# Graph stage: rows of f2 scores by transposing one more column of h1 and h2, in place of 512-column products

## The reference, cut to what matters

```
h = inp @ W
f1 = h @ a[:F, 0]
f2 = h @ a[F:, 0]
e = leaky_relu(f1[:, :, None] + f2[:, None, :], 0.2)   # (+ mask in the second)
att = softmax(e, axis=2)
h_prime = elu(att @ h)

out = relu(x @ mlp1_w + mlp1_b);  res = out
out = elu(gat(out, None, W_fc, a_fc)) + res
out = relu(out @ mlp2_w + mlp2_b);  res = out
out = relu(elu(gat(out, adj, W_hand, a_hand)) + res)
```

## Time and profile before

| | us |
|---|---|
| median of 3 runs | 1116.54 (1116.24 to 1118.69) |
| the profiled execution | 1119.85 |
| its span, first to last instruction | 1118.1 |
| PE busy in the span | 975.7 |
| DVE busy | 737.7 |
| ACT busy | 675.1 |
| POOL busy | 481.2 |

### The profile page before, as it was taken

The page is one execution under the profiler, slowest core; times in us unless marked ns, Lnnn a source line. Parts: engine busy times, 40 slices in busy tenths (PEclk is TensorE's granted clock), DMA queues, the critical chain, the costliest instruction groups (busy, mean ns, idle before and its releaser), DMA issues. The chain is left out here.

```text
span 1118.1 us, 25162 instructions
## 1 busy us (share of the span) xinstructions
PE 975.7 (87%) x7980; PEld 817.2 (73%) x7980; DVE 737.7 (66%) x2234; ACT 675.1 (60%) x1670; POOL 481.2 (43%) x474
## 2 busy tenths in 40 slices
PE   1698999997999999999999925899999998459998
PEld 1577888886667799999999922666666665349997
DVE  4678888885650145555545523588898896569998
ACT  4445666654433446666656613688888887467773
POOL 2545666651154654444400057677766722011111
PEclk9879999999999999999999966999999999779999
DMA  7900100112613137766565411111111100001011
GB/s 201 373 6 32 47 38 38 38 40 77 175 58 121 53 115 206 206 207 201 175 180 176 127 47 47 30 36 30 32 34 29 32 5 1 1 1 39 29 38 47
DMA packets 91705, 94.14 MB, mean 84 GB/s; under 512 B 16336, under 2 KB 69712, under 8 KB 90448
## 3 DMA queue, kind: packets, MB, share of 16 engines
q1 hardware_dynamic: 71936, 50.40, 14.4%
q10 hardware_dynamic: 11472, 25.63, 7.9%
q0 software_dynamic: 8192, 16.79, 4.9%
HBM read 52.54 MB, written 33.96 MB: 77 GB/s over the span
## 5 line engine op out<-in xcount | busy, mean ns | idle before, releaser
L1548 POOL DMA_INDIRECT g_y<-slot_rows_out,slots x128 | 129.6, 1012 | 141.3 <-SPq L1977 92.1
L1283 POOL DMA_INDIRECT slot_rows_in<-xn_all,slots x128 | 129.7, 1013 | 136.8 <-DMA slot_rows_in<-xn_all,slots 93.6
L1170 ACT ACTIVATE s_hT<-s_hp,expert 128x256 f32<-128x256 f32 x284 | 111.8, 476 | 54.6 <-PE s_hp L1161 54.5
L1183 PE MATMUL s_yp<-w_experts,s_hT 128*128 x1136 | 138.0, 275 | 0.0
L1183 PEld LDWEIGHTS s_yp<-w_experts,s_hT 128*128 128x128 f32 x1136 | 132.8, 192 | 0.0
L1191 DVE TENSOR_TENSOR xnT_all<-s_yp,expert 128x256 f32<-128x256 f32 x71 | 30.1, 424 | 117.7 <-PE s_yp L1183 117.7
L489 DVE SCALAR_TENSOR_TENSOR l_mi<-l_sbc,mT 128x512 bf16<-128x512 f32 x128 | 84.5, 670 | 7.1 <-PE l_sbc L480 5.9
L1159 PE MATMUL s_hp<-e_xh,e_wh 128*128 128x256 f32 x284 | 86.6, 305 | 0.0
L1082 ACT ACTIVATE s_hT<-s_hp,b_shared 128x512 f32<-128x512 f32 x64 | 44.0, 687 | 65.3 <-PE s_hp L1065 63.7
L1160 PE MATMUL s_hp<-e_xl,e_wh 128*128 128x256 f32 x284 | 80.5, 284 | 0.0
L1161 PE MATMUL s_hp<-e_xh,e_wl 128*128 128x256 f32 x284 | 80.5, 284 | 0.0
(11 more groups left out here) (323 smaller groups left out, 2652.7 us busy)
## 6 DMA issues: line engine op xcount, KB each, us to landing
expert<-expert_rows ACTq DMA_DIRECT2D x65, 322.0 KB, 3.1
slot_rows_in<-zeros SPq DMA_DIRECT2D x9, 1024.0 KB, 12.8
xnT_all<-slot_rows_in SPq DMA_DIRECT2D x71, 128.0 KB, 3.1
slot_rows_out<-xnT_all SPq DMA_DIRECT2D x71, 128.0 KB, 2.3
xn_all<-l_xr SPq DMA_DIRECT2D x16, 256.0 KB, 2.3
xnT_all<-l_rT SPq DMA_DIRECT2D x16, 256.0 KB
out_dram<-f_ot SPq DMA_DIRECT2D x16, 256.0 KB, 2.3
w_experts<-in_L_ffn_W2p_dram SPq DMA_DIRECT2D x8, 256.0 KB, 3.8
```

Source lines behind the costliest of these rows:

```text
L1170: nc.scalar.activation(hT[q % 2][:, c, :], hp[:, c, 0:TILE], ACT.Gelu, bias=wt[q][:, F + c:F + c + 1]).then_inc(s["h_ok"], 1)
L1183: ins = pe.matmul(yp[q % 2][:, h * D:(h + 1) * D], hT[q % 2][:, c, h * P:(h + 1) * P], w2, start=(c == 0 and h == 0), stop=(c == FC - 1), ...
L1283: pool.indirect_dma_start(k.rows_in, bass.IndirectOffsetOnAxis(ap=k.slots[:, c, b:b + 1], axis=0), k.xn[:, b, :], None).then_inc(scattered ...
L1548: pool.indirect_dma_start(y_slot[c][:, b, :], None, k.rows_out, bass.IndirectOffsetOnAxis(ap=k.slots[:, c, b:b + 1], axis=0))\
```

## The change

The two repeated weight vectors and the DVE copies that filled them go away. `pe_b_h1` makes one more column, so h1 has f2 in column `FD + 1` (258 columns), and `pe_d_h2` likewise (130 columns). A row of f2 scores is now made by a transpose: the column of h1 is read 128 times with stride zero as a 128x128 block, whose transpose has f2 along the free dimension in every partition. There are four such transposes a group in `pe_b_f2`, which wait for the copies of h1 (`h1_ok`), and four in `pe_d_f2`, which wait for the copy of h2 (`h2_ok`). In PE's slot, `pe_d_f2` moves from ahead of `pe_b_sums` to behind it, and `pe_b_f2` from ahead of `pe_d_transpose` to behind `pe_a_dense`. The orders of ACT and DVE stay.

```diff
-    k.w_f2_fc = sb("w_f2_fc", [P, 2, P])
-    k.w_f2_hand = sb("w_f2_hand", [P, P])
...
-                dve.tensor_copy(k.wr_rep[:], k.wr_last[:].to_broadcast([P, P]))
-                dve.tensor_copy(k.w_f2_fc[:], fold_1[:, :, 1:2].to_broadcast([P, 2, P]))
-                fold(dve.tensor_copy(k.w_f2_hand[:], fold_2[:, 1:2].to_broadcast([P, P])))
+                fold(dve.tensor_copy(k.wr_rep[:], k.wr_last[:].to_broadcast([P, P])))
...
-W1C = FD + 1
+W1C = FD + 2
 W1S = FD + 4
-W2C = D + 1
+W2C = D + 2
...
         def pe_b_f2(pe, g, p):
             wait(pe, s["y1_ok"], g)
             wait(pe, s["y2_ok"], g - 1)
-            for c in range(H1):
-                ins = pe.matmul(ff[:], k.w_f2_fc[:, c, :], r1T[p][:, c, :], start=(c == 0), stop=(c == H1 - 1))
+            for b in range(GB):
+                wait(pe, s["h1_ok"], g * GB + b + 1)
+                ins = pe.transpose(ff[:, b * P:(b + 1) * P], h1[p][:, b, FD + 1:FD + 2].to_broadcast([P, P]), k.ident[:])
             ins.then_inc(s["f1_ps"], 1)
...
-                                           bias=h1[p][:, b, FD:W1C])
+                                           bias=h1[p][:, b, FD:FD + 1])
...
         def pe_d_f2(pe, g, p):
             wait(pe, s["y1_ok"], full(lambda n: n, g, 1))
             wait(pe, s["y2_ok"], g)
-            pe.matmul(ff[:], k.w_f2_hand[:], r2T[p][:], start=True, stop=True).then_inc(s["f2_ps"], 1)
+            wait(pe, s["h2_ok"], g + 1)
+            for b in range(GB):
+                ins = pe.transpose(ff[:, b * P:(b + 1) * P], h2[:, b, D + 1:D + 2].to_broadcast([P, P]), k.ident[:])
+            ins.then_inc(s["f2_ps"], 1)
...
-                                           bias=h2[:, b, D:W2C])
+                                           bias=h2[:, b, D:D + 1])
...
             if on["d"]:
                 pe_d_h2(pe, g, p)
-                pe_d_f2(pe, g, p)
             if on["c"]:
                 pe_b_sums(pe, g + 1, q)
+            if on["d"]:
+                pe_d_f2(pe, g, p)
             if on["b"]:
                 pe_b_h1(pe, g + 2, p)
             if on["a"]:
                 pe_a_transpose(pe, g + 3)
-            if on["b"]:
-                pe_b_f2(pe, g + 2, p)
             if on["d"]:
                 pe_d_transpose(pe, g)
             if on["a"]:
                 pe_a_dense(pe, g + 3)
+            if on["b"]:
+                pe_b_f2(pe, g + 2, p)
             if on["c"]:
                 pe_c_dense(pe, g + 1)
```

## The result

The changed kernel took 1209.41 us (median; 1204.38 to 1214.08), the kernel before 1116.39 in the same comparison: 1.085 times as long, 95% interval 1.0773 to 1.0927. The prediction was 1197, range 1174 to 1222.

A forecast was written before the change was run, and what follows sets the result against it. The prediction took a closed DVE and ACT loop in the graph stage as the bound. Order costs of 61.6 us plus 18.9 for clock falls, +80.5 on 1116.5, gave 1197 us, range 1174 to 1222.

The forecast's parts named there:

- The loop: Graph stage: a closed DVE and ACT loop sets the 16.67 us slot; PE's net 1.66 us saving a group gains nothing.
- faster, because TensorE is the bound: Rival: less PE work in 14 groups saves 23.2 us, giving 1093 us; chance 0.02.
- The f1 wait: At act_b_sum: f1's rows, now behind pe_d_transpose and pe_a_dense, make ACT start 3.11 us later, paid in each slot.
- The f2 wait: At act_d_sum: f2's rows, now behind pe_b_sums, delay dve_d_leaky and the copies of h1, taken as 1.2 us a slot.
- Only the f1 wait is on the loop: Rival: DVE comes so late that it covers f2's delay; 43.2 us more, giving 1160; chance 0.06.
- Stride zero: Transposes of the broadcast column: priced like contiguous ones, 0.60 us per four; bounds -15.6 to +12.7 us.
- The clock: Longer PE pauses lower TensorE's granted clock; a fall costs 1.45 us, bounds 0 to 37.7 us, 18.9 taken.
- the two stands where it falls: PE pauses ahead of pe_d_h2, 3.8 us with nothing but transposes, and ahead of pe_a_dense, 3.4 us likewise.
- with one case each way I take half: Clock term: between no fall and two a slot, half of 37.7 us was taken, 18.9.
- The two rows it rested on: Earlier trace: full clock kept after a 2.70 us pause; lost after pauses of 0.71 and 1.43 us around four transposes.
- the clock falls at both pauses: Rival: two falls in every slot add the full 37.7 us, giving 1216 us; chance 0.17.
- The ends: Slots -1, 13, 14 and 15, with only some parts: 1.4, 1.4 + 1.2, 1.2 and 0.4 us more.

The follow-up runs named there:

- both_back: Changed kernel with pe_b_f2 and pe_d_f2 both back at their old places in PE's slot, leaving only transposes for products; 1130.98 us, ratio 1.006 to the kernel before.
- f1_back: Changed kernel with only pe_b_f2 put back ahead of pe_d_transpose; 1164.18 us, ratio 1.0289 to the kernel before.
- dense_first: Changed kernel with pe_a_dense and pe_b_f2 put ahead of pe_d_transpose; 1190.59 us, ratio 1.053 to the kernel before.
- fill_one: Changed kernel with useless products filling only PE's stand ahead of pe_d_transpose, the one ahead of pe_d_r2 left open; 1206.99 us, ratio 1.073 to the kernel before.
- after: The changed kernel itself, as first measured and profiled; 1209.41 us, 1.085 times the kernel before.
- after_again: The changed kernel unaltered, run once more in another series; 1228.1 us, ratio 1.0905 to the kernel before.
- before_again: The kernel before, unchanged, run and profiled once more on another chip; 1120.35 us, against 1117.5 us for the kernel before beside it.
- sum_first: Changed kernel with f1's transposes, then pe_a_dense, ahead of pe_d_transpose, f2 by product at its old place, act_b_sum ahead of act_d_exp; 1124.76 us, ratio 1.0009 to before.
- sum_first_split: The version sum_first with GpSimd's addition u1 cut into two instructions; 1128.47 us, ratio 1.0009 to the kernel before.
- warm: Changed kernel with useless products filling both longer PE stands, ahead of pe_d_transpose and pe_d_r2; 1211.95 us, ratio 1.0681 to the kernel before.
- warm_again: The same kernel as warm, with both longer PE stands filled, run in another series; 1206.05 us, ratio 1.0766 to the kernel before.
- order_only: Kernel before with PE's slot order of the changed kernel, f1 and f2 still made by products; 1244.89 us, ratio 1.0995 to the kernel before.
- f2_back: Changed kernel with only pe_d_f2 put back ahead of pe_b_sums; 1220.35 us, ratio 1.0748 to the kernel before.

## Why the prediction was right or wrong

**The loop.** Right. DVE and ACT's work didn't change, PE's saving was worth nothing (both_back, 1.006: 1.5 us a slot less busy, no gain), and the rival "faster, because TensorE is the bound" has fallen.

**The f1 wait, 3.11 us.** Right: 3.05 on ACT in the full-clock slot, 3.1 by f1_back, made of 1.9 and 1.15 by dense_first.

**The f2 wait, 1.2 us.** Right: 1.29 on ACT and 1.14 on DVE, 1.0 by f2_back and 0.9 between f1_back and both_back. "Only the f1 wait is on the loop" is out: the slot at full clock is 21.03, against 16.67 + 4.31 = 20.98.

**Stride zero.** Right to take the contiguous price. The tile view of the kernel after, min/median/max in ns, has f1's transposes, f2's, and for comparison those of `g_xn`:

```profile
L1624 PE MATMUL g_ff<-ident,g_h x64: 272/273/421, 670.3 to 1024.3; 128*128 128x128 f32 x64
...
L1745 PE MATMUL g_ff<-ident,g_h x64: 272/273/294, 707.2 to 1051.6; 128*128 128x128 f32 x64
```

```profile
L1585 PE MATMUL g_tb<-ident,g_xn x64: 271/272/473, 655.1 to 997.5; 128*128 128x128 f32 x64
```

Each set took 0.60 us at granted clock 1.00, so the 13 us that the rule of the Trainium skill ("TensorE: Matmul & The Clock Gate", Part 4) would have added are not there.

**The clock.** The price of a fall was right (1.45 said, 1.48 between the slots of 21.03 and 22.51), and so were the places of the two stands where it falls. The term that was mis-sized is the count of the falls, "with one case each way I take half", 13 falls for 18.9 us. Of the 89.9 us that the 13 slots grew (307.38 less 217.46), the order takes 13 x 4.31 = 56.0; the 33.9 that are left, over 23 falls, are 1.47 each. The two rows it rested on the earlier trace rows were single stands in a stage that was otherwise full; after the change nearly every slot lost the clock at both places. With only one of them open it was lost there in seven slots of 13 (fill_one), near the half that was taken. The rival "the clock falls at both pauses", 37.7 us, was nearer in mechanism and in size. The third stand, 1.77 us, was not in the forecast; in after no fall begins at it.

**The ends.** 5.6 was said; 4.7 more up to the first slot (60.8 us from the stage's first instruction on PE, against 56.1) and 2.5 in the last two slots (34.0 against 31.5) were measured, 7.2 in all. The stage grew by 97.1 us: 80.5 as forecast, and 15.0 for the falls and 1.6 for the ends.

**The rest.** The stage began 12.2 us earlier in the span than before (655.1 against 667.3), and 0.35 were won behind it, so the span grew by 84.5 and the medians by 93.0. The earlier start is not the change's: the same kernel starts the stage at 667.7 in after_again, and the kernel before at 667.5 in before_again. Where it comes from stays open. By this luck the profiled span came within 4.0 us of the forecast, while the stage, the only part that was forecast, was 16.6 off. The median, on which the forecast was made, is 12.4 above it (1209.41 against 1197). In after_again the kernel took 103.5 us more than the one before beside it, a ratio of 1.0905 where the forecast's is 1.072: the miss is then larger, and in the same direction.

**What stays open.** Why ACT starts `act_d_sum` up to 3.6 us after its input in some kernels, all of its long cases being slots in which the gather runs; and what decides whether a stand of 2.1 us loses the clock, as it did in seven slots of fill_one and not in six.

## What to carry to other kernels

First find the loop that sets the period and ask of each moved instruction what then lies ahead of it in its in-order queue: here it cost the wait and the work of all that it was put behind, 4.3 us a slot, while 1.5 us less work on the busiest engine bought nothing. Then look at TensorE where its work became less, and list its stands. Two of 2.1 to 2.3 us a slot lost the clock 23 times of 26 here, one of 2.1 us with the other filled seven times of 13, and with one of 1.9 and one of 0.8 (both_back) one slot of 13 had a fall: the count goes by the stands of a slot together, not by each alone. Giving them some useless products shows what the clock is worth. Before an operation is moved earlier, look at what the other engines do at that moment.

## What the runs showed of the hardware

VectorE's `dve_b_leaky`, an instruction on 512 elements a partition whose two inputs are both in SBUF, takes 0.69 us, 2.02 when it starts while GpSimd adds two tensors of 1024 (sum_first), and 0.94 when that addition comes in two halves (sum_first_split). It is held rather than slowed: in sum_first it ends 0.54 or 0.55 us after GpSimd's addition (914.03 + 2.67 = 916.70, 915.22 + 2.02 = 917.24) in all 15 groups where the two meet, and in the kernel before, where it meets only the tail of the addition and takes 0.80 to 0.86 us (once 1.48), it ends by the same 0.54 to 0.56 behind it. The instruction ahead of it, 914.62, reads one of its two inputs, `g_rr`, from PSUM and takes 0.69 us under the same addition. The Trainium skill, "GPSIMD Engine Reference", section 1 "Specifications", names contention of GpSimd with VectorE's instructions that read two inputs from SBUF; these rows agree with it, but that the ports are its cause was not shown here.

Useless products keep the clock up and cost nothing where the engine would stand: in warm PE was busy 17.83 us in a slot of 21.02, against 14.39 in after's slot of 21.03. That holds for the slots in which ACT was not late; whether the filling has to do with ACT being late more often in warm than in after_again (seven cases against one) isn't shown.

ACT can stand 2.9 to 4.0 us at an instruction whose input has been there for the last 1.8 to 3.6 of them, the profile giving "remote" as releaser (7 cases in warm, 6 in f1_back, 3 each in fill_one and warm_again, 1 in after_again, none in after, order_only, f2_back, both_back, dense_first and before_again). In the slots of warm where it happens the granted clock is 0.86 to 0.93, so it costs more than its own length.
